# Order of the score matmuls on TensorE: row group by row group instead of in rounds of four row groups

## What is computed

```python
# a full layer, in short (x: 16 x 256 x 256, context: 16 x 120 x 256)
xm = ln(x) * (1 + sc_sa) + sh_sa
q, k, v = split(xm @ qkv_w + qkv_b)                      # 16 heads of 16
x = x + g_sa * (softmax(q k^T * 0.25) v @ proj_w + proj_b)
q = ln(x) @ q_w + q_b;  k, v = split(context @ kv_w + kv_b)
x = x + (softmax(q k^T * 0.25) v @ cp_w + cp_b)
x = x + g_ff * (gelu((ln(x) * (1 + sc_ff) + sh_ff) @ fc1_w + fc1_b) @ fc2_w + fc2_b)
```

## Time and profile before

| | us |
|---|---|
| median of 3 runs | 2756.78 (2750.43 to 2758.21) |
| the profiled execution | 2759.04 |
| its span, first to last instruction | 2757.3 |
| TensorE busy | 2537.3 (92%) |
| TensorE weight loads busy | 1902.8 (69%) |
| VectorE busy | 1835.5 (67%) |
| ScalarE busy | 1253.7 (45%) |
| mean granted TensorE clock | 0.968 of full speed |

### The profile page before, as it was taken

The page is one execution under the profiler, slowest core; times in us unless marked ns, Lnnn a source line. Parts: engine busy times, 40 slices in busy tenths (PEclk is TensorE's granted clock), DMA queues, the critical chain, the costliest instruction groups (busy, mean ns, idle before and its releaser), DMA issues.

```text
span 2757.3 us, 66128 instructions
## 1 busy us (share of the span) xinstructions
PE 2537.3 (92%) x27522; PEld 1902.8 (69%) x27522; DVE 1835.5 (67%) x3543; ACT 1253.7 (45%) x1759; POOL 456.9 (17%) x461
## 2 busy tenths in 40 slices
PE   6778999999999899999999999999999999999987
PEld 5556676666676676666667777777777777777766
DVE  3466667777776777766767666666767766776742
ACT  0324544444444444444454545455454545445442
POOL 0011111111111111111111111121111112121111
PEclk7789999999999999999999999999999999999999
DMA  5322222222222222222212221222222221222210
GB/s 179 101 74 75 69 70 75 79 75 75 69 69 67 84 69 80 77 78 86 65 58 63 79 65 58 86 67 81 73 98 81 73 82 60 85 63 85 71 35 31
DMA packets 236652, 207.54 MB, mean 75 GB/s; under 512 B 87634, under 2 KB 221973, under 8 KB 236357
## 3 DMA queue, kind: packets, MB, share of 16 engines
q1 hardware_dynamic: 236356, 203.32, 23.5%
HBM read 58.34 MB, written 4.39 MB: 23 GB/s over the span
## 4 chain that ended last, share of the span: by engine, by line
PE 70%; DVE 17%; issue 6%; ACT 4%; DMA 1%; SPq 1%; POOL 1%; POOLq 0%; DVEq 0%; ACTq 0%
PE ring L1237 12%; PE ring L1115 11%; PE o_acc L1205 9%; PE score L1175 8%; DVE row_max_F L858 7%; PE score L1153 7%; PE ring L1227 7%; PE ring L1217 4%; DVE row_max_G L858 4%; PE score L1180 3%; PE ring L1134 3%; PE ring L1014 2%; PE ring L1137 2%; PE ring L1123 2%; ACT probs L994 1%
## 5 line engine op out<-in xcount | busy, mean ns | idle before, releaser
L994 ACT ACTIVATE probs<-score 120x2048 f32<-120x2048 f32 (+1 forms) x320 | 601.7, 1880 | 364.1 <-PE score L1180 355.8
L858 DVE TENSOR_REDUCE row_max_F<-score 128x8 f32<-128x2048 f32 x192 | 437.9, 2281 | 42.1 <-PE score L1153 41.9
L1227 PE MATMUL ring<-x_t_E,w_fc 128*128 128x256 f32 x1536 | 381.3, 393 | 0.0
L1237 PE MATMUL ring<-w_fc,h_t 128*128 128x256 f32 x1536 | 375.3, 398 | 1.0 <-ACT h_t L1005 1.0
L1005 ACT ACTIVATE h_t<-ring,cols 128x256 f32<-128x256 f32 x384 | 161.3, 471 | 430.7 <-PE ring L1227 430.7
L1237 PEld LDWEIGHTS ring<-w_fc,h_t 128*128 128x128 f32 x1536 | 294.5, 198 | 62.0 <-issue 18.6
L1227 PEld LDWEIGHTS ring<-x_t_E,w_fc 128*128 128x128 f32 x1536 | 278.2, 190 | 67.8 <-issue 19.1
L880 DVE STREAM_TRANSPOSE o_turned<-o_acc 128x512 f32<-128x512 f32 x224 | 159.7, 713 | 205.6 <-PE o_acc L1205 205.6
L858 DVE TENSOR_REDUCE row_max_G<-score 128x16 f32<-128x1920 f32 x128 | 275.7, 2154 | 28.3 <-PE score L1153 28.3
L741 DVE SCALAR_TENSOR_TENSOR k_parts<-ring,cols,k_parts 128x256 fp32r<-128x256 f32 (+1 forms) x224 | 79.9, 398 | 234.6 <-ACT k_parts L976 234.5
L976 ACT ACTIVATE k_parts<-ring,cols 128x256 fp32r<-128x256 f32 (+1 forms) x224 | 79.6, 406 | 297.3 <-PE ring L1115 224.7
(11 more groups left out here) (133 smaller groups left out, 3798.6 us busy)
## 6 DMA issues: line engine op xcount, KB each, us to landing
q_G<-q_parts SPq DMA_DIRECT2D x256, 128.0 KB, 2.1
q_F<-q_parts SPq DMA_DIRECT2D x192, 128.0 KB, 2.1
k_F<-k_parts SPq DMA_DIRECT2D x96, 256.0 KB, 2.5
k_F<-k_parts SPq DMA_DIRECT2D x192, 128.0 KB, 2.2
k_G<-k_parts SPq DMA_DIRECT2D x128, 120.0 KB, 2.2
k_G<-k_parts SPq DMA_DIRECT2D x256, 60.0 KB, 1.9
gate_now_P<-gate_rows SPq DMA_DIRECT2D x48, 256.0 KB, 3.6
gate_now_E<-gate_rows SPq DMA_DIRECT2D x48, 256.0 KB, 3.8
```

Of the source, the lines that this page charges most:

```text
L858: nc.vector.tensor_reduce(dst, src, AX.X, ALU.max).then_inc(row_max_ready[r].sem, 1)
L994: nc.scalar.activation(probs[v % 2][0:keys, :, :], score[0:keys, :].rearrange("p (h q) -> p h q", h=2 * GROUPS), ACT.Exp, scale=SCALE).the ...
L1227: last = mm(ps[:, c % 2 * NT:(c % 2 + 1) * NT], w_fc1[:, k, c * P:(c + 1) * P], x_t[r][:, k, :], start=k == 0, stop=k == KC - 1)
L1237: last = mm(ps[:, 0:D], h_t[:, k, t * P:(t + 1) * P], w_fc2[:, k, :], start=k == 0, stop=k == MC - 1)
```

## The change

Inside an S step, for each head e, the loop over the groups g goes outside the loop over the parts: group 0 gets its two matmuls, then group 1 its two, and so on. Inside a T step the selector matmul moves into the same loop: group 0 gets its three matmuls, then group 1 its three. The instructions are the same ones in the same number; the order within one row group is the same as before; the last matmul of a step is the one of group 3 in both kernels, with the same increment; no wait and no other step is touched.

```diff
                         for e in range(2):
-                            for two in range(2):
-                                for g in range(GROUPS):
-                                    at = slice(32 * g, 32 * (g + 1))
+                            for g in range(GROUPS):
+                                at = slice(32 * g, 32 * (g + 1))
+                                for two in range(2):
                                     col0 = g * BANK + (e * NT if r == "F" else (2 * c + e) * S)
                                     last = mm(score[:, col0:col0 + width],
...
                     for e in range(2):
-                        for two in range(2):
-                            for g in range(GROUPS):
-                                at = slice(32 * g, 32 * (g + 1))
+                        for g in range(GROUPS):
+                            at = slice(32 * g, 32 * (g + 1))
+                            for two in range(2):
                                 mm(score[0:keys, g * BANK + e * NT:g * BANK + (e + 1) * NT],
                                    k_now[at, two, c, e, tile * P:tile * P + keys].bitcast(F32R),
                                    q_now[at, c, e, :].bitcast(F32R), start=two == 0, stop=False)
-                        for g in range(GROUPS):
-                            at = slice(32 * g, 32 * (g + 1))
                             last = mm(score[0:keys, g * BANK + e * NT:g * BANK + (e + 1) * NT],
                                       sel[at, 2 * c + e, 0:keys].bitcast(F32R), max_t[r][at, :].bitcast(F32R),
                                       start=False, stop=True)
```

## The result

| | before | after |
|---|---|---|
| median of the runs, us | 2756.78 (7 runs, 2750.43 to 2760.08) | 2765.94 (7 runs, 2758.77 to 2773.37) |
| ratio, 95% interval | | 1.0043 (1.0024 to 1.0062) |
| profiled execution: span, us | 2757.3 | 2763.4 |
| busy TensorE, us | 2537.3 | 2541.9 |

The account below looks back on a forecast made before the run. TensorE, busy 92% of the span, was taken as the bound. Growth of S (5 to 10 ns) and T (12 to 20 ns), 320 steps each, gave 5.4 to 9.6 us, taken as 7.5: 2756.8 + 7.5 = 2764 us; range 2745 to 2805.

Parts of the forecast that it names:

- Row groups are queued as column groups are: S and T steps: TensorE passes a group's blocked matmuls, so four groups still run abreast; 7.5 us slower, chance 60%.
- signs that the prediction named: T step 0.98 to 1.0 us, F's S step 0.75 to 0.77, four starts within 30 ns, score lines' busy growth under 10 us.
- Rival 1: S and T steps: matmuls start strictly in program order across row groups; 395 to 585 us slower, chance 20%.
- upper bound: G's S step under strict program order: 16 x 0.11 - 0.84 = +0.94 us a step, 120 us in all.
- The skew: S and T steps: group 3's first pair stands later in the stream, 3.3 ns a pair; S +10 ns, T +20 ns.
- lower bound: Part of the skew already exists at a step's end (18 ns, not 10): only S +5, T +12 ns; 5.4 us.
- forecast's own range: Whole kernel, if TensorE passes blocked matmuls: 2757 to 2770 us.
- Each nanosecond counts as one: Each nanosecond an S or T step grows lengthens the end time equally; one on both is 0.64 us over 320 steps each.
- Rival 2: T steps: TensorE passes too few blocked instructions, losing one 0.117 us round a step; 37 us, 2802 us total, chance 12%.
- Rival 3: S and T steps: rounds get up to 9 ns cheaper when four no longer meet; 19.6 us won, 2745 us, chance 8%.
- Same or slower: Verdict against no change, told apart at about 0.3%, 8.3 us: faster 6%, same 40%, slower 54%.

Follow-up runs that it names:

- eight of G's S in a row: Against the kernel before, only G's S steps changed: all eight matmuls of a row group follow each other; 2991.68 us, ratio 1.0868.
- S alone: Against the kernel before, only the S steps take the change's group-by-group order, T as before; 2758.10 us, ratio 1.0014.
- four of F's S in a row: Against the kernel before, only F's S steps changed: all four matmuls of a row group follow each other; 2760.05 us, ratio 1.0019.
- T alone: Against the kernel before, only the T steps take the change's group-by-group order, S as before; 2761.98 us, ratio 1.0028.
- the first round: As the changed kernel, but each S and T step begins with one matmul of each row group; 2762.20 us, ratio 1.0028 against the kernel before.
- six in a row: Against the kernel before, only T changed: all six matmuls of a row group follow each other; 3109.61 us, ratio 1.1293.
- five in a row: Against the kernel before, only T changed: five matmuls of a row group follow each other, then one, group by group; 2984.35 us, ratio 1.0828.
- F's S in one row group: Against the kernel before, only F's S steps changed: all 16 matmuls read row group 0, four banks written as before; 2984.45 us, ratio 1.0840.

## Why the prediction held, point by point

**Row groups are queued as column groups are.** This was the chosen step. Four groups start within 30 ns in a T step of the changed kernel (median of F; 34 ns in G) though each group's second and third matmul stand between them in the stream. The reading of the PV step, with two instructions of one column group directly behind each other, was the right evidence; that it carries over from column groups to row groups was assumed, and the runs bear it out. The signs that the prediction named came too: the T step takes 0.99 us to the end of its records (0.98 to 1.0 were named), F's S step 0.76, and the busy time of the three lines grows by 7.9 us (under 10). Rival 1, strict order, falls with it. The rule that the prediction took from the Trainium skill ("TensorE: Matmul & The Clock Gate", Part 3, "The mechanism"), that matmuls start in program order, does not hold for matmuls of different row groups in these runs: group 0's third matmul of a T step starts behind group 3's second. The rival built like it had 20% and was 395 to 585 us above the kernel before, where 9.2 were measured. Its price for G's S step was left between nothing and its upper bound, on the ground that a matmul of 120 columns is about half as long; with eight of G's S in a row the first group's matmuls start 111 ns apart, against 118 with 256 columns, so the upper bound was the right one.

**The skew.** +10 ns for S and +20 ns for T were read from the PV step's 20 ns against 10 and from 3.3 ns a pair. Measured: 10, 9, 20 and 22 ns. The points further out fit: 13th pair, 40 to 44 ns.

**The size.** The term that was mis-sized is the lower bound. I took one T step's last round, 18 ns apart, for the usual one and let it eat half of the gain in skew. Over all T steps of F the skew of the last four has a median of 10 ns, as that of the first four (14 and 10 in G), and the whole added skew is paid: 9.7 us in the steps instead of the 7.5 that I took. One step of 192 was too few to read a median from. The time, 2765.9 against 2764, is within the forecast's own range; that the two lie only 2 us apart, where single runs scatter by 5, is partly luck.

**Each nanosecond counts as one.** True within the error for the change, for S alone (2.9 in, 3.0 out) and for four of F's S in a row (6.1 in, 6.2 out); T alone and the first round came out 1.7 and 2.7 us above their steps. For steps that grow by over a microsecond it isn't: TensorE's idle time fell by 35 us where the steps grew by 191, and by 45 where they grew by 273.

**Rival 2** had a real mechanism with a wrong count. A reach exists, but it is counted per row group and ends behind three waiting matmuls; I had counted instructions over all groups and looked for the loss at the seam between the two heads. The change has one (S) or two (T) waiting behind a group's first: it stays one matmul short of the most that is passed. With six in a row the time would have been 3110.

**Rival 3**, a round that gets cheaper when four no longer meet: rounds stay at 0.117 us, and no order tried is faster than the kernel before.

**Same or slower.** The prediction gave slower 54% and same 40%. Of the 54, 32 were for rivals 1 and 2, which didn't occur, so "slower" was more likely on paper than its right mechanism made it. With the full skew of 9.7 us the change lies just beyond 0.3%, and two sets of runs agree on 1.0043.

## What to carry to other kernels

If matmuls of several row groups are to run abreast, the order in which they are issued matters little here (0.2 to 0.4% of this kernel) as long as no group has more than four in a row; each instruction pair ahead of the last group's first costs 3.3 ns once a step. Beyond that the other groups stand idle while one works off its queue, and the cost rises from nanoseconds to two thirds of a microsecond a step with five in a row. The edge was measured between four and five with 256 columns; with 120 columns only eight in a row was run, and its step fits the same count. To judge such a reordering, look for a place in the same trace where two instructions of one tile are already neighbours (each plain float32 matmul here is such a pair), and count starts in narrow windows instead of reading durations.

## What the runs showed of the hardware that I had not expected

- The edge between three and four waiting matmuls of one row group: steps of 734 against 1382 ns for four and five in a row, and it is sharp enough to predict 1370 and 2330 ns from one trace.
- Eight of G's S in a row brings the lower clock with it. The kernel before has 0.98 and 1.00 in its two middle stretches. With steps in which 32 matmuls of 120 columns take 2.3 us, one or two row groups at a time, they read, by stretch:

```profile
400.00:1400.00 1000.00, 954.69 (x9630) 733.48 (x9629) 656.81 (x1262) 429.48 (x612) 153.61 (x154) 0.96 0.22 69
1400.00:2400.00 1000.00, 971.56 (x9837) 741.30 (x9836) 636.06 (x1201) 459.52 (x631) 159.15 (x154) 0.97 0.22 68
```

TensorE's busy time is no lower than before (955 and 972 us of 1000, before 923 and 970), and still the lower level was granted for more of the time. In the clock record of this trace 32 stretches at the lower level begin between 400 and 2400 us, and 29 of them begin 2.2 to 3.7 us after the start of one of G's S steps, that is at its end or just behind it; the kernel before has 10 such stretches there. That few row groups work at a time isn't enough by itself, though. With F's S in one row group, where 16 matmuls of 256 columns take 1.9 us one by one, the same stretches read:

```profile
400.00:1400.00 1000.00, 953.57 (x10023) 736.19 (x10021) 685.85 (x1317) 445.54 (x637) 163.96 (x162) 0.99 0.23 71
1400.00:2400.00 1000.00, 975.16 (x9637) 757.90 (x9630) 626.09 (x1176) 449.46 (x619) 156.06 (x152) 1.00 0.21 67
```

and T steps with five or six in a row have 0.98 to 1.00 there. What sets the steps with 120 columns apart was not tested. What the runs show is that a stretch can be as full in busy time and yet be granted the lower level more often.
